# A differential-attention and mixture-of-experts block on one core: norms moved into the lead, routing behind it, two slots weighed in one piece

## The reference, cut to what matters

```
x: (8, 512, 128) f32;  xn = layernorm(x)
attention, H=8 heads of 16, each with two maps of 8:
    qs, ks = (xn @ Wq.T), (xn @ Wk.T) as (b, s, 8, 2, 8);  vs = (xn @ Wv.T) as (b, s, 8, 16)
    att = softmax(scores[map 0]) - diff_weight * softmax(scores[map 1])
    o = att @ vs;  o = o * rsqrt(mean(o*o over heads and dims) + eps) * norm_w
    out_a = (o @ Wo.T + bo) * (1 - diff_weight)
experts: gates = sigmoid(xn @ Wg), top 2 of 8, weights divided by their sum
    h = silu(xn @ W1) * (xn @ W3);  y = h @ W2        (inner size 256; the shared one and the 2 chosen)
    out_f = (shared + weighted sum of 2) / 3
result = x + out_a + out_f
```

## Time and profile before

| | us |
|---|---|
| median of 3 timed runs (lowest, highest) | 683.73 (679.42, 683.97) |
| the profiled execution's own time | 677.72 |
| its span in the profile | 675.9 |
| mean granted TensorE clock | 0.956 |

### The profile page before, as it was taken

One profiled execution on the slowest core, in us unless ns is written; L12 is line 12 of the kernel. 1 busy time (PEld: TensorE's weight loads), 2 busy tenths in 40 slices (PEclk: granted clock), 3 DMA queues, 4 the chain that ended last, 5 costly groups with the idle time before them and its releaser, 6 DMA issues.

```text
span 675.9 us, 11161 instructions
## 1 busy us (share of the span) xinstructions
PE 620.1 (92%) x3570; PEld 326.6 (48%) x3570; DVE 478.9 (71%) x1025; ACT 401.4 (59%) x782; POOL 243.6 (36%) x328
## 2 busy tenths in 40 slices
PE   6698989999999999999999989999999989999894
PEld 5244444455454544555455445545545545545321
DVE  5788868788777877677666666667667666777274
ACT  3004655656566656666667656666666656666772
POOL 7304450257667740232233322223323223323211
PEclk8556989999999999999999999999999999999997
DMA  3717459121313123152433315142241422210292
GB/s 105 203 55 135 48 97 146 13 75 41 104 40 112 48 92 96 46 168 71 116 93 101 106 46 156 61 143 79 76 134 58 137 76 81 83 46 13 68 254 66
DMA packets 54754, 62.26 MB, mean 92 GB/s; under 512 B 7048, under 2 KB 38792, under 8 KB 54696
## 3 DMA queue, kind: packets, MB, share of 16 engines
q1 hardware_dynamic: 49832, 51.68, 29.7%
q0 software_dynamic: 4544, 9.35, 4.3%
q10 hardware_dynamic: 320, 0.52, 0.3%
HBM read 27.50 MB, written 16.59 MB: 65 GB/s over the span
## 4 chain that ended last, share of the span: by engine, by line
PE 70%; DVE 16%; issue 7%; ACT 3%; DMA 1%; POOL 1%; SPq 1%; DVEq 0%; ACTq 0%
PE F L1059 16%; PE O L1025 14%; PE ST L1011 13%; PE F L1071 9%; PE S L992 6%; DVE rowmax L750 6%; DVE hid L781 4%; DVE ub L772 3%; PE F L926 2%; PE F L931 1%; PE F L922 1%; PE F L963 1%; PE ST L992 1%; PE F L1043 1%; PE F L979 1%
## 5 line engine op out<-in xcount | busy, mean ns | idle before, releaser
L750 DVE TENSOR_REDUCE rowmax<-S 128x1 f32<-128x512 f32 x490 | 323.7, 682 | 157.6 <-PE S L992 156.9
L586 ACT ACTIVATE probs<-ST 128x512 f32<-128x512 f32 x490 | 265.8, 595 | 81.7 <-PE ST L1011 77.9
L992 PE MATMUL S<-kop,qop 62*128 62x512 f32 x490 | 196.6, 475 | 8.2 <-DMA kop<-kparts 3.5
L1011 PE MATMUL ST<-qop,kop 64*128 64x512 f32 x490 | 181.8, 450 | 8.3 <-ACT probs L586 5.2
L1025 PE MATMUL O<-probs,vop 128*32 128x512 f32 x1024 | 148.2, 612 | 0.1
L421 POOL DMA_INDIRECT yt<-ysb,xst x78 | 76.6, 982 | 120.8 <-DMA yt<-ysb,xst 106.6
L1011 PEld LDWEIGHTS ST<-qop,kop 64*128 64x128 f32 x490 | 74.0, 187 | 79.0 <-issue 37.3
L992 PEld LDWEIGHTS S<-kop,qop 62*128 62x128 f32 x490 | 80.7, 191 | 26.5 <-DVE rowmax L750 21.4
L380 POOL TENSOR_SCALAR o_inv<-o_inv,ndw 128x8 f32<-128x8 f32 x32 | 10.2, 319 | 201.5 <-DVE o_inv L796 201.3
L1059 PE MATMUL F<-xsT,wrt_all 128*128 128x256 f32 x312 | 76.6, 388 | 2.2 <-ACT xsT L567 1.2
L410 POOL DMA_INDIRECT xs<-xn,slot_i x64 | 62.1, 971 | 25.3 <-DVE rowmax L750 16.0
(11 more groups left out here) (141 smaller groups left out, 559.9 us busy)
## 6 DMA issues: line engine op xcount, KB each, us to landing
wrt_all<-in_wexp SPq DMA_DIRECT2D x39, 384.0 KB, 3.1
qop<-qparts SPq DMA_DIRECT2D x64, 128.0 KB
kop<-kparts SPq DMA_DIRECT2D x60, 128.0 KB
xs<-xst SPq DMA_DIRECT2D x13, 387.0 KB, 10.8
xst<-xs SPq DMA_DIRECT2D x39, 129.0 KB, 2.9
base<-in_x SPq DMA_DIRECT2D x8, 256.0 KB, 4.1
xn<-yt SPq DMA_DIRECT2D x8, 256.0 KB, 5.0
out_x<-base SPq DMA_DIRECT2D x8, 256.0 KB, 2.7
```

Source lines behind the costliest of these rows:

```text
L586: A(probs[:, n % NP, :], st_bank(n)[:, :], ACT.Exp, scale=SCALE).then_inc(s_p, 1)
L750: V.reduce_max(rowmax[hf][:, 1 - k % 2, q // 2 % HC, (2 * q + k // 2) % QT:(2 * q + k // 2) % QT + 1], s_bank(n)[:, :], AX).then_inc(s_mx, 1)
L992: mm(s_bank(n)[:, :], qop[b % 2][at:at + TERMS, c, t * P:(t + 1) * P], kop[b % 2][at:at + TERMS, c, :], start=True, stop=True, tile_positi ...
L1011: mm(st_bank(n)[:, :], kop[b % 2][at:at + BAND, c, t * P:(t + 1) * P], qop[b % 2][at:at + BAND, c, :], start=True, stop=True, tile_positio ...
```

## The change

1. **Norms.** All statistics are taken before the loop: `ln_stats(2)` before `residue_q(0)`, `ln_stats(3)` to `(7)` after `residue_k(0)`. One power and one `ln_bias` serve batches 2 to 7. ScalarE normalises them in slots -11 to -6; `do_xT` and `do_z` follow in slots -9 to -3. The constants move from VectorE to GpSimd, and the clearing of `qop[1]`, `kop[1]` there goes behind constants and power. q and k of batch 1 and v of batch 0 move ahead of the loop.
2. **Routing** starts at slot 0, `do_prefix` at slot 4, the scatters at slot 8 (2 or 3 a slot). Seven of the 13 fills of `xs` are issued before slot 0.
3. **Tiles** stand at every even slot from 6 to 114, the shared ones first. Both halves of `up` still stand together at the end of the (now always even) slot; `xsT` is at the end of the odd slot before, `down` at that of the odd slot behind. tanh, `gate_u` and `gate_hid` work in `hid`; `tb` and `ub` go.
4. **Weighing**: both `weigh(slot - 2)` and `weigh(slot - 1)` after k step 1 of an even slot; `probs` has 12 buffers instead of 8.
5. **Small groups** stand behind k step 3 in even slots, before `up`, and behind k step 1 in odd ones. proj moves to s=8 (after k step 1), q to 8, k to 10, v to 12, `squares`, `add_proj` and the residues to even slots, each behind the row maximum of k step 1. ScalarE copies q and k twice, so that the bank is free without VectorE. `max_parts` comes one slot later, in one piece; the maxima's rows are laid by two DMAs instead of four.
6. All x are loaded before the small inputs and the layouts. `combine` of the last batch comes before the last slots' end.

```diff
-    SH_AT = [10 + 2 * i for i in range(SH_TILES)]
-    RT_AT = [43 + 71 * r // (RT_TILES - 1) for r in range(RT_TILES)]
-    TILE_AT = SH_AT + RT_AT
+    RT_AT = [38 + 2 * r for r in range(RT_TILES)]
+    SH_AT = [at for at in range(6, SLOTS, 2) if at not in RT_AT][:SH_TILES]
+    TILE_AT = sorted(SH_AT + RT_AT)
...
-    LN_AT = [None, None, 0, 1, 3, 4, 6, 7]
-    PREFIX_AT = 14
-    SCAT0 = 18
-    FILL0, FILLS, FILL_ROWS = 2, 13, 6
+    NORM_AT = [None, None] + [x - 13 for x in range(2, BATCH)]
+    PREFIX_AT = 4
+    SCAT0 = 8
+    FILLS, FILL_ROWS = 13, 6
+    FILL_AT = [-10, -9, -8, -6, -5, -4, -3, 1, 2, 3, 4, 5, 6]
...
+    def rest(slot):
+        return 3 if slot >= 0 and slot % 2 == 0 else 1
...
             def lay_m(n):
                 par, hf = n // 2 % 2, n % 2
                 sp.wait_ge(s_mc, n + 1)
-                for a in range(PARTS):
-                    for h in range(2):
-                        at, src = h * BAND + TERMS + a, (a * 2 + h) * HC
-                        sp.dma_start(qop[par][at:at + 1, HC * hf:HC * hf + HC, :].bitcast(f32),
-                                     mrows[n % 2][src:src + HC, :]).then_inc(s_ml[hf], 16)
+                for h in range(2):
+                    at, src = h * BAND + TERMS, h * PARTS * HC
+                    sp.dma_start(qop[par][at:at + PARTS, HC * hf:HC * hf + HC, :].bitcast(f32),
+                                 mrows[n % 2][src:src + PARTS * HC, :]).then_inc(s_ml[hf], 16)
...
-                if s == 9 and 1 <= b + 2 < BATCH:
+                if s == 13 and 1 <= b + 2 < BATCH:
...
+            ln_pow(2, BATCH)
+            G.memset(qop[1][:, :, :].bitcast(f32), 0.0).then_inc(s_pads, 1)
+            G.memset(kop[1][:, :, :].bitcast(f32), 0.0).then_inc(s_pads, 1)
...
-                A(qparts[:, 0, :], F[1 if b == 0 else 2][:, :], ACT.Copy).then_inc(s_q1, 1)
+                bank = F[1 if b <= 1 else 2]
+                A(qparts[:, 0, :], bank[:, :], ACT.Copy).then_inc(s_q1, 1)
+                if b >= 1:
+                    A(qparts[:, 1, :].bitcast(f32), bank[:, :], ACT.Copy).then_inc(s_qf, 1)
...
                 for k in range(4):
                     if 0 <= slot < SLOTS:
                         exp_tile(slot, k)
+                    j = tile_at(slot)
+                    if j is not None and k == 3:
+                        tanh_half(j)
...
             residue_k(0)
...
+            for b in range(3, BATCH):
+                ln_stats(b)
+            ln_bias(3, 2, BATCH)
...
                 for k in range(4):
                     if 0 <= slot < SLOTS:
                         score_exp(slot, k)
                     if slot + LEAD < SLOTS:
                         score_max(slot + LEAD, k)
                     if k == 1:
-                        if 1 <= slot <= SLOTS:
+                        if 2 <= slot <= SLOTS and slot % 2 == 0:
+                            weigh(slot - 2)
                             weigh(slot - 1)
-                        other(slot)
+                        if s == (8 if b < BATCH else 4) and b >= 1:
+                            do_proj(b - 1)
...
+                    if k == rest(slot):
...
+                        other(slot)
+                    j = tile_at(slot)
+                    if j is not None and k == 3:
+                        up(j, 0)
+                        up(j, 1)
+                    if k == 3:
+                        r = routed(tile_at(slot + 1))
                         if r is not None:
                             do_xsT(r)
-                    if k == 3:
                         j = tile_at(slot - 1)
                         if j is not None:
                             down(j)
-                        j = tile_at(slot)
-                        if j is not None:
-                            up(j, 0)
-                            up(j, 1)
```

More of the change, by code:

```diff
@@ L490, in _ @@
                 if slot >= SCAT0:
[L491 removed]
+                    for i in range(2 + slot % 2):
                         if scat < TOPK * NT:
@@ L878, in _ @@
-                    if k == 2:
+                    at = slot + LEAD - (1 if slot >= 0 else 0)
+                    n = at // 8 - 1
+                    if at % 8 == 0 and 0 <= n < 2 * BATCH and k == (1 if slot >= 0 else 0):
+                        for i in range(3):
+                            max_parts(n, i)
+                    if k == 1:
+                        if s == 4 and 1 <= b < BATCH:
+                            squares(b - 1)
+                        if s == 8 and 1 <= b < BATCH:
+                            add_proj(b - 1)
+                        if s == 10 and 1 <= b + 2 < BATCH:
+                            residue_q(b + 2)
+                        if s == 12 and 1 <= b + 2 < BATCH:
+                            residue_k(b + 2)
@@ L889, in _ @@
-                        if s == 4 and b >= 1:
-                            if b == BATCH:
-                                combine(b - 1, True)
-                            add_proj(b - 1, b == BATCH)
-                    if k == 3:
+                        if s == 2 and b == BATCH:
+                            squares(b - 1)
+                        if s == 4 and b == BATCH:
+                            add_proj(b - 1)
                         if slot in COMBINE_AT:
-                            combine(COMBINE_AT.index(slot), False)
+                            combine(COMBINE_AT.index(slot))
```

255 lines of the change are left out of this document (121 added, 134 removed).

## The result

The changed kernel takes 661.66 us (median of 4 runs, 660.15 to 663.33) where the kernel before takes 682.55 (4 runs, 679.42 to 683.97): a ratio of 0.970, 95% interval 0.966 to 0.975. Forecast were 667 us and "faster by over 1%". So the spans differ by 15.4 us and the medians by 20.9. The account by steps is made on the spans. A second trace of the kernel before (e9, 683.41 us, span 681.5) shows where its executions differ: slots 0 to 5 take 31.0 us there instead of 27.4, slots 6 to 115 take 545.3 instead of 542.1.

What follows compares the result with a forecast made beforehand. TensorE, busy 92% of the span, was taken to bound the kernel. Lead +7.0, slots 0 to 5 -2.9, body -19.6 and end -0.8 gave -16.3, so 667 us from the median 683.73; range 654 to 684.

Steps and rivals of the forecast that it cites:

- The odd slot: Body: VectorE's queue sets its length, down done at U+5.52; a pair of slots without a small group takes 8.72 us.
- The step with the wrong sign: Body, even slots: weighing two slots in one piece takes 1.87 us instead of 1.00 each, 1.86 used in the sum.
- The body's size: Slots 6 to 115: 522.5 us against 542.1, a change of -19.6 us.
- The 3 us for q, k and v: Body: second copies on ScalarE stand behind tanh and delay oT and exponentials, 3 us in all (bounds 0 and 8).
- the 2 us for the maxima's rows: Body: rows of maxima come late where ScalarE is behind, 2 us for 15 half batches (bounds 0 and 15).
- rival B: Body: maxima's rows land late behind a tile's weights, stalling each half batch 2.3 us; 700 or 692 us, slower; chance 9%.
- Rival A: Body: the stall only moves, VectorE's six passes bind odd slots and even slots lose again; 682 to 686 us; chance 18%.
- Slot 0: Lead: starts at 62 us against 55.03 (+7) by SP's queue of fills, 58.5 by the compute path; bounds 58.5 and 66.
- The term that was too small: Lead: six gate products taken the same as six transposes (1.05 us at half clock); both together 4 us at slot 0.
- Slots 0 to 5: 24.5 us against 27.4 (-2.9): VectorE's row maxima and routing steps 21.3, half clock 1, stall 2.2; bounds 22 and 28.
- Rival C: Lead: fills do not delay slot 0 (58 instead of 62) and the clock is up; 659 to 662 us; chance 20%.
- The end: Slots 117 to 128: paired weighings save 2.4 us, last weighing +0.9, late maxima rows +0.7; in sum -0.8 us.

Runs made afterwards that it cites:

- e9: The kernel before, unchanged, run once more for its trace on a chip of the later runs; 683.41 us.
- e2: The changed kernel with tanh's first product (gate_u) behind the first row maximum again, as before the change; 703.49 us, ratio 1.014 to the kernel before.
- e1: The changed kernel with one slot weighed in every slot again instead of two in even slots; 638.02 us, ratio 0.919 to the kernel before.
- e3: The changed kernel with the seven early fills of xs issued only in slot 0; 671.18 us, ratio 0.970 to the kernel before.
- e4: The changed kernel with routing four slots later and three scatters a slot; 667.61 us, ratio 0.961 to the kernel before.
- e5: The changed kernel itself once more, beside the kernel before on one more chip; 674.71 us, ratio 0.969 to the kernel before.
- e8: The changed kernel with one weighing in every slot and routing four slots later; 649.51 us, ratio 0.937 to the kernel before.
- e10: The changed kernel with the small groups behind k step 1 in even slots too; 667.42 us, ratio 0.978 to the kernel before.
- e11: The changed kernel with one weighing in every slot and three scatters in every slot; 627.24 us, ratio 0.920 to the kernel before.
- e6: The kernel before with tanh's first product (gate_u) ahead of the slot's first row maximum; 675.52 us, ratio 0.972 to the kernel before.

## Why the prediction was right, and where not

**The odd slot.** "Counting from the start U of `up`", VectorE's queue was to end `down` at U + 5.52. Measured: `up` takes 1.92 and the odd slot 3.66, so U + 5.58, and the wait before `down` is 0.19 as given. The pair without a group was forecast at 8.72 and is 8.76; the hidden oT is there too (224.54 to 228.20 has an oT and is 3.66 long). e2 confirms the mechanism: its first product begins 1.18 us behind the start of the slot (349.87) where the changed kernel's begins 0.12 ahead of it (215.66), the second product begins 2.38 behind it instead of 1.78, and the slot is longer by these 0.60. This is the step on which the sum rested, and it held.

**The step with the wrong sign is the weighing**: "One weighing takes 1.00 here ... two in one piece should be 1.87", a gain of 0.13 a pair. The 1.85 came, and it was a saving of 4.4 us of weighing for 18.4 us of scores in slots 42 to 105. The forecast had the odd slot's end from VectorE alone, and its own sentence, "TensorE's own work from U+1.93 is only 2.71 us, so 0.88 us are idle, the same stall as before", holds the answer. Before, the slot took 4.26 us for 3.40 of TensorE's work, the weighing among it, and 0.86 were a stall. The product's new place alone shortens the slot to 3.66 with the same work (e1), and 0.26 are left of the stall. The pairing took 1.00 of work out of the slot and left its length at 3.66, so the stall was there again, as room for the weighing that had just been moved; groups of 0.59 fill five of its eight places. The sum was not hurt, as it described the changed kernel; what it credited was.

**The body's size**, -26.2 for -19.6. The 3 us for q, k and v and the 2 us for the maxima's rows did not come: no `score_exp` of slots 8 to 112 has a listed wait for `mrows`; only slot 0 (3.3) and slot 120 (3.0) wait, and the odd slots of s = 9 are 3.66 us long like the others. That is rival B's place, and it fell with them. The rest, 1.6, is 0.3% of the stretch. Rival A, a stall that only moves, did not come: even slots of the changed kernel without a group take 5.12, odd ones 3.66. e2 shows how near it was: with the product behind, the gain is gone.

**Slot 0**, 64.03 for 62, within its bounds, but mostly by the other path. The queue alone was to bring the rows at 62, with the compute path done at 58.5. The rows landed 2.72 (e2) to 4.75 us behind their last issue, and without early fills slot 0 still begins at 61.99 (e3). The compute path begins as forecast, with the first row maximum at 27.03 (forecast 27.3) after a power of 4.18 us (forecast 4.0), and ends at 61 to 62. The term that was too small is the gate product: "I take the same" as a transpose, 1.05 at half clock; the chain shows 1.80 each (the row at 33.87), six of them 4.5 us more. The prediction set the start of 62 beside the Trainium skill (DMA: Bandwidth & Descriptors, Queues, rings and completion order), by which each DMA engine consumes the descriptors of a ring in their order. These traces neither show nor refute that rule; with the fills ahead of them the rows lost 0.9 to 2.9 us against the 1.85 of the earlier trace rows, and of that up to 2 us reached slot 0.

**Slots 0 to 5**, 28.1 for 24.5. The count of VectorE's steps was to give 2.5 us in slot 0, 1.3, 0.6 and 2.2 of stall, and "the first slots at half clock 1". But TensorE was busy 24.9 of the 28.1 us and VectorE 20.5 (the row of 64.03:92.17 above), at a mean clock of 0.71: the work that the forecast left out is TensorE's own at half clock. The clock was 0.5 until 77 us, 13 us behind the start of slot 0, and again in two stretches before slot 10, where the forecast had one us for it. With the routing steps out of the first four slots 24.0 us are left (e4), where the forecast without them had 14.4 for VectorE and 1 for the clock. That the clock falls so early could be read in the earlier trace rows: the prediction has it at 0.5 in the second to fourth slices and at 1.0 from there on, where the row has 0.6, 0.9 and 0.8 in the fourth to sixth. Rival C, fills that do not delay slot 0 and a clock that is up in the lead, was right in no more than its first half. How large the miss is hangs on the trace: e5 has 29.8 us for the 28.1, e9 31.0 for before's 27.4.

**The end**, +1.1 for -0.8. The timeline of TensorE in the last slots, the second row being the weighing behind slot 120's first scores, the third a later one at full clock:
```profile
621.17 0.79 PE L1026 MATMUL ST<-qop,kop 64*128 64x512 f32 x2 [2.98 <-DMA qop<-mrows]
621.89 3.64 PE L1040 MATMUL O<-probs,vop 128*32 128x512 f32 x16
...
630.04 1.92 PE L1040 MATMUL O<-probs,vop 128*32 128x512 f32 x16
```
Slot 120 waits 2.98 us for the maxima's rows, where the price was +0.7, and the granted clock is 0.5 from then to 626 us, so that the weighing takes 3.64 instead of 1.92. The saving by pairs was larger than forecast, as a pair takes 1.92 where 4.1 less 0.45 were counted; the wait and the clock took it back.

## What to carry to other kernels

When work is moved out of a slot, ask first what its engine would otherwise wait for there: work that lies in another engine's shadow costs nothing, and the same work in a slot that TensorE fills costs all of its length. Two ways of shortening one stall (a shorter queue on VectorE, more cover on TensorE) are not to be added up, and are tested as a table of two by two and not one by one. Where two banks alternate between a producer and a consumer, back-to-back groups of the producer can take longer than the listed wait says, since matmuls that ran side by side come apart (2.41 us for 1.34 here); ask which list sets the length of the slot before you count that as a loss. And when a sum comes out right, compare its terms: here an edit that costs 15 us stood inside a forecast that was met.

## What the runs showed of the hardware

**Common pauses of ScalarE and VectorE, on some chips.** The traces of e1 to e8, on two chips, have between 120 and 240 us some places (two in e2, six in e5) where ScalarE or VectorE, mostly both, stand still for 2 to 4 us and start again together, while TensorE works on until it waits for them; before, changed, e9, e10 and e11 have none. They come in slots 12, 16, 20, 24, 28 or 32, or just behind: every fourth slot, the one in which O is copied to oT. e5 is the changed kernel itself, and by chance its slots 14 to 16 begin within 0.02 us of those of the first trace, so one of its pauses can be set beside the same work without it. Timeline of the first trace, then of e5:
```profile
145.53 1.92 PE L1040 MATMUL O<-probs,vop 128*32 128x512 f32 x16
...
147.52 0.60 ACT L558 ACTIVATE oT<-O 128x512 f32<-128x512 f32 x1 [1.04 <-PE O L1040]
...
147.95 1.29 DVE L775 TENSOR_REDUCE rowmax<-S 128x1 f32<-128x512 f32 x2 [1.23 <-PE S L1007]
```
```profile
145.52 1.92 PE L1040 MATMUL O<-probs,vop 128*32 128x512 f32 x16
...
150.40 0.60 ACT L558 ACTIVATE oT<-O 128x512 f32<-128x512 f32 x1 [3.93 <-remote]
150.47 1.29 DVE L775 TENSOR_REDUCE rowmax<-S 128x1 f32<-128x512 f32 x2 [3.76 <-remote]
```
The weighing ends at the same time in both; the copy of O and the row maximum behind it begin 2.9 and 2.5 us later in e5. The bracket "remote" says that the profile found no releaser, so whether TensorE's signals came late or something else held both engines is not shown. In e5 slots 26 to 41 take 80.2 us for 74.5, and the whole program 674.7 for 661.7; the kernel before takes 694 to 695 us on these chips and 683 on the others. Since before has them too (by its time, and by e6), the ratio of the change is 0.969 on the one kind and 0.970 on the other. The cause is open. All pauses fall while scatters to `xs` are issued, but the same scatters run without a pause on the other chips.

**The power's cost goes by columns.** Four columns took 1.02 us on GpSimd, 24 take 4.18: (4.18 - 1.02) / 20 is 0.16 us a column, which leaves 0.39 us of each instruction as start-up: an estimate from these two sizes. One piece of 24 saves 1.9 us against six of 4.

**A matmul of eight columns is not cheap at half clock.** The gate product streams 8 columns for every 128 of its stationary operand and takes 1.80 us for 8 matmuls, more than four transposes of 128 columns (0.95 in the chain). In the rows of the weight loads its eight loads take 1.78 us and the transposes' four 0.90, so each costs 0.22 us whether 8 or 128 columns are streamed behind it.
